# A decoder kernel's head: x loaded first, quaternion weights loaded once, biases combined in one row, 20 idle products

## The reference, cut to what matters

```python
def quat_linear(x, W, b):                       # W: 4 x 64 x 64, b: 4 x 64
    xs = x.reshape(B, T, 4, D4)
    A = jnp.einsum('btcd,wdo->btcwo', xs, W) + b
    r = A[:, :, 0, 0] - A[:, :, 1, 1] - A[:, :, 2, 2] - A[:, :, 3, 3]
    ...                                          # i, j, k with other signs and pairs
    return jnp.concatenate([r, i, j, k], axis=-1)
q = quat_norm(quat_linear(x, qW, qb))
k = quat_norm(quat_linear(x, kW, kb))
v = quat_linear(x, vW, vb)
scores = einsum(q, k) * scale + jnp.mean(jnp.sin(J[:T])) * 0.1
attn = softmax(scores); out = quat_linear(attn @ v, oW, ob)
x = _layernorm(x + out)
```

## Time and profile before

| | |
|---|---|
| time, median of 3 runs | 780.7 us (780.52 to 780.96) |
| the profiled execution's own time | 774.46 us |
| its span | 772.7 us |
| PE busy | 698.3 us, 90% of the span |
| ACT busy | 557.5 us, 72% |
| DVE busy | 492.1 us, 64% |
| POOL busy | 193.3 us, 25% |

### The profile page before, as it was taken

One profiled execution on the slowest core, in us unless ns is written; L12 is line 12 of the kernel. 1 busy time (PEld: TensorE's weight loads), 2 busy tenths in 40 slices (PEclk: granted clock), 3 DMA queues, 4 the chain that ended last, 5 costly groups with the idle time before them and its releaser, 6 DMA issues.

```text
span 772.7 us, 10924 instructions
## 1 busy us (share of the span) xinstructions
PE 698.3 (90%) x3854; PEld 383.6 (50%) x3854; DVE 492.1 (64%) x1156; ACT 557.5 (72%) x1071; POOL 193.3 (25%) x234
## 2 busy tenths in 40 slices
PE   4999999989999999989999999967988999993897
PEld 2652222212222223879888887633454644441686
DVE  4794645663422133669527666767887787988786
ACT  3759999999999997464242434799987633799991
POOL 1661143210110000203352232455554200000022
PEclk9999999999999999999999999999999999997899
DMA  7412112241157142203156000002000000000002
GB/s 195 140 31 49 30 28 69 28 96 28 28 111 230 29 115 77 102 8 111 46 172 215 5 0 1 1 1 82 7 35 1 1 1 0 1 0 0 1 27 82
DMA packets 58606, 42.27 MB, mean 55 GB/s; under 512 B 38226, under 2 KB 55352, under 8 KB 58424
## 3 DMA queue, kind: packets, MB, share of 16 engines
q1 hardware_dynamic: 58408, 41.44, 19.5%
q10 hardware_dynamic: 144, 0.13, 0.1%
HBM read 28.72 MB, written 4.46 MB: 43 GB/s over the span
## 4 chain that ended last, share of the span: by engine, by line
PE 55%; ACT 24%; DVE 15%; issue 3%; DMA 1%; SPq 1%; POOL 0%; POOLq 0%; ACTq 0%; DVEq 0%
ACT arena L665 12%; PE banks L1673 9%; PE banks L2210 8%; PE banks L1972 7%; PE banks L1988 6%; PE banks L1659 4%; ACT arena L790 4%; PE banks L1643 3%; DVE arena L1498 2%; DVE arena L1063 2%; PE banks L1833 2%; PE banks L1646 2%; DVE arena L1071 2%; PE banks L2002 1%; PE banks L1716 1%
## 5 line engine op out<-in xcount | busy, mean ns | idle before, releaser
L665 ACT ACTIVATE arena<-banks 128x1024 f32<-128x1024 f32 x256 | 239.8, 1047 | 6.7 <-PE banks L1673 4.2
L1673 PE MATMUL banks<-arena 128*32 128x512 f32 x1024 | 136.4, 604 | 2.6 <-DVE arena L1139 2.4
L1659 PE MATMUL banks<-arena 64*128 64x512 f16 x512 | 86.4, 383 | 10.3 <-ACT arena L665 5.8
L2210 PE MATMUL banks<-arena 128*128 128x512 f32 x192 | 83.1, 594 | 1.1 <-DVE arena L1514 0.9
L790 ACT ACTIVATE arena<-banks,arena 128x77 f32<-128x77 f32 x256 | 70.6, 403 | 13.9 <-DVE arena L1413 13.7
L414 POOL TENSOR_SCALAR arena<-arena 128x2 f32<-128x2 f32 (+2 forms) x39 | 11.8, 302 | 254.9 <-DVE arena L1066 254.9
L1659 PEld LDWEIGHTS banks<-arena 64*128 64x128 f16 x512 | 21.0, 93 | 108.8 <-ACT arena L665 98.9
L746 ACT ACTIVATE arena<-banks,arena 128x256 f32<-128x256 f32 x64 | 26.9, 471 | 49.3 <-PE banks L1972 49.3
L2210 PEld LDWEIGHTS banks<-arena 128*128 128x128 f32 x192 | 36.2, 190 | 47.4 <-issue 43.4
L1988 PE MATMUL banks<-arena 128*128 128x256 f32 x256 | 56.5, 380 | 1.2 <-ACT arena L687 1.2
L1972 PE MATMUL banks<-arena 128*128 128x256 f32 x256 | 56.2, 379 | 0.0
(11 more groups left out here) (255 smaller groups left out, 1253.4 us busy)
## 6 DMA issues: line engine op xcount, KB each, us to landing
arena<-in_L_ffn_w SPq DMA_DIRECT2D x16, 1024.0 KB, 7.5
w_kept<-arena SPq DMA_DIRECT2D x3, 768.0 KB, 3.6
arena<-w_kept SPq DMA_DIRECT2D x3, 768.0 KB, 4.4
arena<-in_x SPq DMA_DIRECT2D x4, 512.0 KB, 7.1
out_x<-arena SPq DMA_DIRECT2D x3, 512.0 KB, 2.9
arena<-in_L_ffn_b SPq DMA_DIRECT2D x1, 1024.0 KB, 14.9
arena<-in_L_ffn_w_gate SPq DMA_DIRECT2D x1, 768.0 KB, 7.6
arena<-in_L_ffn_w_up SPq DMA_DIRECT2D x1, 768.0 KB, 9.4
```

The source lines that it names most:

```text
L665: act.activation(PT[kt % 2][:, half], PS[:, 2 * (n % 3):2 * (n % 3) + 2, :], ACT.Exp, scale=DH ** -0.5 / QK_UP ** 2).then_inc(sem("exp_don ...
L1659: mm = pe.matmul(bank(2 * (n % 3) + h), KT[u % 2][64 * h:64 * h + 64, P * kt:P * kt + P], QT[u % 2][64 * h:64 * h + 64, 512 * half:512 * h ...
L1673: mm = pe.matmul(PS[32 * j:32 * j + 32, 6, :], VS[w][:, kt, h, :], PT[kt % 2][:, half, h, :], start=(kt == 0), stop=(kt == TB - 1))
L2210: mm = pe.matmul(bank(2 + n % 4), (wgT if n < IC * G4 else wuT)[:, k, P * c:P * c + P], XT[:, k, 512 * g:512 * g + 512], start=(k == 0), s ...
```

## The change

Six edits, all but one in the first 60 us of the program:

1. SP issues the first four tiles of x first, and then each weight array once, to partitions 0 to 63. ACT now unfolds its half by reading partitions 0 to 63 and writing partitions 64 to 127.
2. The four bias arrays are loaded to one partition, by four transfers that ACT issues ahead of the one for J.
3. POOL sums the biases on that one partition (12 instructions of 4 x 64 elements), where DVE did it on 128. PE broadcasts the row with two products of one row by 512 columns, and DVE copies the two banks to `bq4`.
4. PE runs ten products of 128 x 128 with the identity ahead of the first turn of x, and ten more behind the broadcast, whose results nothing reads.
5. ACT's sine and its exponential move from the head to t = 9 of the projections, where they take the place of the one-element exponential.
6. `low_part` and `late_low` on POOL compute q and k in one instruction where there were two.

```diff
@@ sync
-            for m, w in enumerate(("qW", "kW", "vW", "oW")):
-                for half in range(2):
-                    sp.dma_start(wraw[64 * half:64 * half + 64, m],
-                                 a["L0_attn_" + w].rearrange("w d o -> d w o")).then_inc(sem("quat_w_in"), 16)
             for g in range(G4):
                 sp.dma_start(X[:, 4 * g:4 * g + 4, :], xf[:, 4 * g:4 * g + 4, :]).then_inc(sem(f"x_in{g}"), 16)
                 if g == 0:
-                    for m, b in enumerate(("qb", "kb", "vb", "ob")):
-                        sp.dma_start(braw[:, m].rearrange("p w o -> p (w o)"),
-                                     row(a["L0_attn_" + b].rearrange("w o -> (w o)")).to_broadcast([P, D])).then_inc(sem("quat_b_in"), 16)
+                    for m, w in enumerate(("qW", "kW", "vW", "oW")):
+                        sp.dma_start(wraw[0:64, m], a["L0_attn_" + w].rearrange("w d o -> d w o")).then_inc(sem("quat_w_in"), 16)
@@ gpsimd
+            pool.memset(bias_ones, 1.0).then_inc(sem("quat_b_row"), 1)
+            pool.wait_ge(sem("quat_b_in"), 16 * 4)
+            for n, c in enumerate((1, 2, 3)):
+                for o in range(NQ):
+                    dst = bias_row[:, :, DQ * o:DQ * o + DQ]
+                    ins = pool.tensor_tensor(dst, dst if n else braw[0:1, :, o, :], braw[0:1, :, c ^ o, :],
+                                             ALU.add if sgn(c, o) > 0 else ALU.subtract)
+                ins.then_inc(sem("quat_b_row"), 1)
+                if n < 2:
+                    pool.wait_ge(sem("quat_b_row"), n + 2)
@@ gpsimd, low_part and late_low
-                for m in range(2):
-                    hi, lo = (QKH[:, m, u0:u0 + NP, t % TB, part, :] for part in range(2))
-                    ins = pool.tensor_tensor(lo, src[:, m], hi, ALU.subtract)
-                ins.then_inc(sem("qk_lo"), 1)
+                hi, lo = (QKH[:, :, u0:u0 + NP, t % TB, part, :] for part in range(2))
+                pool.tensor_tensor(lo, src, hi, ALU.subtract).then_inc(sem("qk_lo"), 1)
@@ scalar
+            for m, b in enumerate(("qb", "kb", "vb", "ob")):
+                act.dma_start(braw[0:1, m].rearrange("p w o -> p (w o)"), row(a["L0_attn_" + b].rearrange("w o -> (w o)"))).then_inc(sem("quat_b_in"), 16)
             act.dma_start(Jb, row(a["L0_attn_J"]).to_broadcast([P, D])).then_inc(sem("j_in"), 16)
-            act.wait_ge(sem("j_red"), 1)
-            act.activation(Jk, Jb, ACT.Sin, accum_out=jred).then_inc(sem("j_sin"), 1)
-            act.wait_ge(sem("j_sin"), 1)
-            act.activation(ec, jred, ACT.Exp, scale=0.1 / D).then_inc(sem("j_exp"), 1)
-            act.wait_ge(sem("quat_w_in"), 16 * 8)
+            act.wait_ge(sem("quat_w_in"), 16 * 4)
...
-                    ins = act.activation(Wq4[64:128, c // 2, :, DQ * o:DQ * o + DQ], wraw[64:128, :, c ^ o, :], ACT.Copy, scale=sgn(c, o))
+                    ins = act.activation(Wq4[64:128, c // 2, :, DQ * o:DQ * o + DQ], wraw[0:64, :, c ^ o, :], ACT.Copy, scale=sgn(c, o))
@@ scalar, t == TB + 1
-                    act.wait_ge(sem("j_exp"), 1)
-                    act.activation(jred, jred, ACT.Exp)
+                    act.wait_ge(sem("j_red"), 1)
+                    act.activation(Jk, Jb, ACT.Sin, accum_out=jred).then_inc(sem("j_sin"), 1)
+                    act.wait_ge(sem("j_sin"), 1)
+                    act.activation(ec, jred, ACT.Exp, scale=0.1 / D).then_inc(sem("j_exp"), 1)
@@ vector
-            dve.wait_ge(sem("quat_b_in"), 16 * 4)
-            for n, c in enumerate((1, 2, 3)):
-                for o in range(NQ):
-                    dst = bq4[:, :, DQ * o:DQ * o + DQ]
-                    ins = dve.scalar_tensor_tensor(dst, braw[:, :, c ^ o, :], sgn(c, o), dst if n else braw[:, :, o, :], ALU.mult, ALU.add)
...
+            dve.wait_ge(sem("quat_b_all"), 1)
+            dve.tensor_copy(bq4.rearrange("p m d -> p (m d)"), PS[:, 6:8, :].rearrange("p a b -> p (a b)")).then_inc(sem("quat_b"), 1)
@@ tensor
+            def running(n):
+                for _ in range(n):
+                    pe.matmul(bank(5)[:, 0:P], ident, ident, start=True, stop=True)
+            running(STARTING)
             x_turn(0)
+            pe.wait_ge(sem("quat_b_row"), 4)
+            for half in range(2):
+                mm = pe.matmul(bank(6 + half), bias_ones, bias_row[:, 2 * half:2 * half + 2].rearrange("p m d -> p (m d)"), start=True, stop=True)
+            mm.then_inc(sem("quat_b_all"), 1)
+            running(STARTING)
             pe.wait_ge(sem("quat_w"), 1)
             pe.wait_ge(sem("quat_w_upper"), 1)
```

More of the change, by code:

```diff
@@ L94 @@
 WARMING = 10
+STARTING = 10
 G2_AT = 17
@@ L219, in decoder @@
         qk_sb = {t: waiting[t - TB] if TB <= t < HT else ringed[t % 3] for t in range(T)}
+        bias_ones = OSB[0:1, 0, 0:P]
+        bias_row = OSB[0:1, 6:8].rearrange("p a (b d) -> p (a b) d", b=2)
         sq = [prj(2 * D) for _ in range(2)]
@@ L921, in _ @@
             dve.tensor_scalar(Jb, Jb, 3.1415925, -3.1415925, ALU.min, ALU.max).then_inc(sem("j_red"), 1)
-            dve.wait_ge(sem("quat_w_in"), 16 * 8)
+            dve.wait_ge(sem("quat_w_in"), 16 * 4)
             for c in (0, 2):
@@ L927, in _ @@
             ins.then_inc(sem("quat_w"), 1)
-            dve.wait_ge(sem("quat_b_in"), 16 * 4)
-            for n, c in enumerate((1, 2, 3)):
-                for o in range(NQ):
-                    dst = bq4[:, :, DQ * o:DQ * o + DQ]
-                    ins = dve.scalar_tensor_tensor(dst, braw[:, :, c ^ o, :], sgn(c, o), dst if n else braw[:, :, o, :], ALU.mult, ALU.add)
-                if n < 2:
-                    link(ins)
-            ins.then_inc(sem("quat_b"), 1)
+            dve.wait_ge(sem("quat_b_all"), 1)
+            dve.tensor_copy(bq4.rearrange("p m d -> p (m d)"), PS[:, 6:8, :].rearrange("p a b -> p (a b)")).then_inc(sem("quat_b"), 1)
             dve.wait_ge(sem("quat_b"), 1)
```

## The result

The changed kernel takes 786.84 us, median of 7 runs (784.55 to 788.84), against 780.7 us (776.4 to 782.78): the ratio is 1.0103, 95% interval 1.0074 to 1.0131. Run once more beside the experiments it took 784.88 us, ratio 1.0080 (1.0054 to 1.0105). By the two ratios it is 8 and 6 us slower, where +4.3 (785.0) was forecast. The median itself lies in the forecast's range of 780.3 to 787.4; 780.7 us times the first ratio, 788.7, lies outside it.

A forecast was written before the change was run, and what follows sets the result against it. Up to 12.03 us transfers and small steps, then PE alone, were taken to bound the head. +3.5 us (clock cases weighted) and +1.0 (sine) made +4.5 on 780.7: 785.2, written as 785.0; range 780.3 to 787.4.

The forecast's parts named there:

- The row on POOL: In the head, POOL's twelve additions at 0.68 us each: bias row ready at 12.5 us, PE waiting 3.5 us.
- Broadcast, ten products, turn, projection: PE's work behind the bias row, through project(0): 6.7 us at 2.4 GHz; first scores +1.7 or +4.7, weighted +3.5.
- If it did rise, 3.5 us of waiting would probably not take it away: In the head, a full PE clock reached before the wait for the bias row would probably survive that wait.
- The wait of 3.67 us late in the kernel: PE idle time after 714.70 us in the profile before, which did not take the full clock away.
- It rises some 6 us after PE starts again: Behind the bias row, PE at 1.2 GHz would reach 2.4 GHz after 6 us; project(0) ends at 22.2.
- the likelier case: PE at 1.2 GHz when the bias row is ready at 12.5 us: project(0) +4.7 us, weighted 0.6.
- The sine: ACT's added block at t = 9 delays x_evac(11), so that project(11) waits: +1.0 us.
- The low halves: POOL's one instruction for two, behind 77 us idle: nothing, up to 0.2 us either way.
- half clock: Upper clock case, PE at 1.2 GHz behind the bias row: 4.7 + 1.0 = +5.7 us, 786.4.
- POOL's upper bound: Bias sum in the head at 12 x 0.73 us and two waits, 9.0 us: +0.8 in the range.
- the late landing: Transfers in the head arriving late: +1 us at the upper end of the range.
- To take it off DVE is worth nothing by itself: In the head, DVE's bias sum is late, but the chain never passes through it: moving it alone gains nothing.

The follow-up runs named there:

- the two later traces: The kernel before, unchanged, traced twice more: 780.75 and 780.84 us, first scores at 57.4 and 58.0.

## Why the prediction was right and wrong

- **Direction and place** held. POOL's row paces the head, PE waits for it, ACT's block at t = 9 delays project(11).
- **The row on POOL** was mis-sized by 1.5 us: it was ready at 13.97, not 12.5. The transfers were there at 4.69 instead of 4.3, and an addition took 777 ns against the 680 that I chose. The first four additions, mostly ahead of DVE's first instruction at 6.59, took 2.83 us, the next two groups of four, beside DVE, 3.19 and 3.04. Whether DVE is the reason stays open: no run has the sum on POOL without DVE at work. The Trainium skill's "GPSIMD Engine Reference", section 3.1, by which I had estimated 0.56 us, was farther off still.
- **Broadcast, ten products, turn, projection** is the step that failed. It was summed as 6.7 us at full clock or 9.7 at half with a rise after 6 us; measured are 3.77 + 4.22 + 0.22 + 2.58 = 10.8, against the weighted 8.5: 2.3 us. "If it did rise, 3.5 us of waiting would probably not take it away": it did rise, near 8, and was gone 2.8 us after PE's last product (2.6 in the second trace), so that the forecast's own wait of 3.5 us would have lost it too. The wait of 3.67 us late in the kernel, on which this rested, was no rule. "It rises some 6 us after PE starts again": it took 7.5 us in this trace, with 3.77 us of one-row products at their beginning; with 128 rows in their place it took 2.9. The forecast saw no difference between the two kinds of product. That the clock was half at the row was forecast as the likelier case, but by luck: the reason given was that the first spell of work is too short for a rise, and the clock rose in it, after some 4 us; it was half because the wait lost it again.
- **The sine** cost 1.3 us, not 1.0: the wait was right, the slower start behind it missing.
- **The low halves** were put at nothing, because POOL had 77 us idle before them. That row is of a later stage; in the head the single instruction went with a wait of 0.4 us at `project(9)`.
- These make 1.5 + 2.3 + 0.3 + 0.4 = 4.5 us, which with the forecast's 4.5 is 9.0, against 8.9 us between the two first traces.
- **The range** was summed too short: half clock, POOL's upper bound and the late landing are 786.4 + 0.8 + 1.0 = 788.2, not 787.4.
- **"To take it off DVE is worth nothing by itself"** was read from one trace, in which `x_evac(2)` was done 0.1 us before its products. In the two later traces the late sum makes PE wait 2.26 and 2.80 us, and project(2) behind it takes 1.8 us longer at the lower clock; as `project(0)` and `project(1)` had been 1.6 us ahead there, first scores stand 2.5 to 3.1 us later. That fits the times: the trace of before suggests +8.9, but against first scores at 57.4 and 58.0 the change costs 5.8 to 6.4, and the second measurement is +6.2. What it would bring to take the sum off DVE and change nothing else, no run shows.
- **DVE beside POOL** was not in the sum: the unfolding ended at 14.52, not near 9.5. That is even 0.55 us behind the row; it did no harm because PE had the broadcast and the second ten products to do until 21.8. The rows show 1.70 us for the unfolding alone and 4.33 beside POOL. The Trainium skill's "SBUF — State Buffer", section "Who interferes with whom", says that `tensor_scalar`, the instruction of the unfolding, can enter a mode in which DVE and GpSimd take the same port pair and one holds it for a whole instruction. The rows agree with a wait of that kind.

The executions of the two first traces differ by 13.0 us, 4.1 more than their first scores. That rest goes with the clock behind the head, which no run isolates: the first trace of before had a mean granted clock of 0.986, that of the change 0.968, and 93 other runs of the kernel before 0.970 to 0.986 with a median of 0.974. It was a lucky execution, 774.46 us, and no base for a fine sum.

## What to carry to other kernels

Moving work to fewer partitions does not shorten it, so a combination "on one row" saves transfers but not engine time; give it to the faster engine and keep it off the stream of the one that paces the stage. Idle products paid only where the engine would have waited anyway and no long wait followed. A broadcast by TensorE that must not lose the clock is safer with full rows, zeros if need be; the traces point that way and do not prove it. Before calling a late step "off the path", look at how early its consumers' last input was: a slack of 0.1 us in one trace was a wait of 2.3 and 2.8 us in the next two.

## What the runs showed of the hardware that I had not expected

- Behind a short wait, one-row products (1 x 512) let TensorE's clock fall in the midst of work: at 12.6 us in one trace and near 11.7 in another, and in neither counterpart with 128 rows.
- Twelve additions of 256 elements take DVE 4.33 us on one partition, and its twelve multiply-and-adds on 128 take 4.37; POOL's additions take 9.2 us on one.
- DVE's eight scalings of 64 x 256 take 1.70 us alone and 4.33 beside POOL's additions.
- Four bias broadcasts of 128 KB put ahead of x and behind J moved x's arrival by 2 to 2.7 us, and the weights' by 3.5.
